# A selective scan on one core: two of sixteen products per sequence move from VectorE to GpSimd

## What is computed

```
xc = silu(causal depthwise convolution of in_proj(chunk))      # 128 channels
dt = softplus(...xc...);  B, C = projections of xc             # 16 states each
A  = -exp(A_log)
for t in range(L):
    h = exp(dt[t] * A) * h + (dt[t] * xc[t]) * B[t]            # 128 channels x 16 states
    y[t] = sum over states of h * C[t]
out = out_proj((y + xc * D) * silu(z))
```

## Time and profile before

| | before |
|---|---|
| median of three runs | 4575.1 us |
| span of the profiled execution | 4583.2 us |
| VectorE busy | 4234.4 us |
| GpSimd busy | 3430.4 us |
| ScalarE busy | 2572.6 us |
| TensorE, matmuls | 3800.3 us |
| mean granted TensorE clock | 0.921 |
| DMA moved | 752.46 MB, mean 164 GB/s |

### The profile page before, as it was taken

One profiled execution on the slowest core, in us unless ns is written; L12 is line 12 of the kernel. 1 busy time (PEld: TensorE's weight loads), 2 busy tenths in 40 slices (PEclk: granted clock), 3 DMA queues, 4 the chain that ended last, 5 costly groups with the idle time before them and its releaser, 6 DMA issues. The chain is left out here.

```text
span 4583.2 us, 51269 instructions
## 1 busy us (share of the span) xinstructions
PE 3800.3 (83%) x13584; PEld 1249.4 (27%) x13584; DVE 4234.4 (92%) x3519; ACT 2572.6 (56%) x3144; POOL 3430.4 (75%) x2085
## 2 busy tenths in 40 slices
PE   3787888888788887988888888888888878888886
PEld 2222323223232222322223232222322223232221
DVE  2699998999999999999999999999999999999997
ACT  2465565655556565565655656555565655656553
POOL 2577777777778787787777877777787777878775
PEclk8898998989999898998989999898999989989998
DMA  1567575675757757576675756757576675766764
GB/s 45 142 158 189 142 197 151 178 184 143 179 148 188 180 154 181 150 183 169 174 179 145 192 146 184 187 138 192 136 186 172 162 181 145 188 160 176 189 160 115
DMA packets 217783, 752.46 MB, mean 164 GB/s; under 512 B 27400, under 2 KB 28816, under 8 KB 213392
## 3 DMA queue, kind: packets, MB, share of 16 engines
q1 hardware_dynamic: 217488, 748.91, 63.3%
HBM read 639.75 MB, written 75.50 MB: 156 GB/s over the span
## 5 line engine op out<-in xcount | busy, mean ns | idle before, releaser
L590 POOL TENSOR_TENSOR state<-state,c_all 128x1024 f32<-128x1024 f32 x1024 | 2399.3, 2359 | 368.8 <-DVE state L960 348.8
L960 DVE TENSOR_TENSOR_SCAN state<-dtb,ub 128x1024 f32<-128x1024 f32 x1024 | 2341.0, 2286 | 51.6 <-ACT dtb L764 5.9
L1184 PE MATMUL ub<-u,spr 64*128 64x512 f32 x4096 | 1313.2, 698 | 454.5 <-DVE state L960 428.8
L764 ACT ACTIVATE dtb<-dtb,a_neg 128x1024 f32<-128x1024 f32 x1024 | 1154.5, 1141 | 537.3 <-DMA dtb<-dt_scratch 480.2
L951 DVE TENSOR_TENSOR ub<-ub,b_all 128x1024 f32<-128x1024 f32 x1024 | 1242.0, 1213 | 63.0 <-issue 30.3
L1184 PEld LDWEIGHTS ub<-u,spr 64*128 64x128 f32 x4096 | 357.4, 199 | 1288.7 <-DVE state L960 887.8
L1200 PE MATMUL yp<-state,gat 128*32 128x512 f32 x4096 | 607.3, 668 | 6.1 <-POOL state L590 6.1
L1053 PE MATMUL mb<-xs,wtap 128*128 128x512 f32 x512 | 244.4, 620 | 19.2 <-DMA xs<-xn 10.6
L657 ACT ACTIVATE e_x<-mb,col 128x512 f32<-128x512 f32 x128 | 88.0, 688 | 259.2 <-PE mb L1067 259.2
L665 ACT ACTIVATE dt<-mb 128x512 f32<-128x512 f32 x128 | 76.2, 595 | 279.4 <-PE mb L1084 279.1
L1067 PE MATMUL mb<-xc,wdt 128*128 128x512 f32 x256 | 160.5, 713 | 58.1 <-DVE ym L841 38.7
(11 more groups left out here) (130 smaller groups left out, 4657.6 us busy)
## 6 DMA issues: line engine op xcount, KB each, us to landing
dtb<-dt_scratch SPq DMA_DIRECT2D x1024, 512.0 KB, 4.8
xs<-xn SPq DMA_DIRECT2D x128, 256.0 KB, 5.2
b_all<-bc_scratch SPq DMA_DIRECT2D x64, 512.0 KB, 6.3
c_all<-bc_scratch SPq DMA_DIRECT2D x64, 512.0 KB, 7.7
xt<-in_x SPq DMA_DIRECT2D x16, 1024.0 KB, 6.9
x_scratch<-xt SPq DMA_DIRECT2D x16, 1024.0 KB, 6.9
dt_scratch<-dt SPq DMA_DIRECT2D x64, 256.0 KB, 3.4
dt_scratch<-dt SPq DMA_DIRECT2D x128, 128.0 KB, 3.7
```

The costliest lines, as they stand in the source:

```text
L590: pool.tensor_tensor(v, v, c_all[:, c % 2, :], ALU.mult).then_inc(gated, 1)
L764: act.activation(dtb[:, k, :], dtb[:, k, :], ACT.Exp, scale=a_neg[:, GROUP[g]:GROUP[g] + 1]).then_inc(decayed, 1)
L960: dve.tensor_tensor_scan(state[:, g % STATES, :], dtb[:, k, :], ub[:, g % 2, :], 0.0, ALU.mult, ALU.add).then_inc(scanned, 1)
L1184: last = pe.matmul(ub[:, g % 2, h * HALF:(h + 1) * HALF], spr[lo:lo + TURN, GROUP[g] % 8, :], u[lo:lo + TURN, c % 2, h * HALF:(h + 1) * HA ...
```

## The change

Units 6 and 14 of each sequence (`POOLED`) no longer use TensorE's spread and VectorE's multiply. SP stores u of their 8 channels into a new scratch in HBM at step 27 of the sequence before (`store_u`, four DMAs of 16 KB), and loads it back repeated for the 16 states into a new buffer `bxs` in SBUF (`load_pooled`): for unit 6 in slot 0, for unit 14 in slot 6, after the scan that read `bxs` last. GpSimd multiplies `bxs` by B in place, after gate 4 for unit 6 and after gate 12 for unit 14. The decay of these units is written to the free half 0 of `ub` in PSUM and not in place, which it may only do when unit 4 or 12 has been scanned; so the scan reads the decay from PSUM and the product from SBUF. `made` counts the multiplies that VectorE still makes, for the semaphores. The diff, its unchanged lines cut:

```diff
SEQ_STEPS = 2 * NU
+POOLED = (6, 14)
 NT = L // P
...
 POOL_SEQ = {3: ["prep_clamp_x"], 5: ["prep_silu_x"], 16: ["prep_dd"], 24: ["own_clamp_z"], 31: ["own_silu_z"]}
-SP_SEQ = {19: ["prep_bc_store"], 22: ["prep_bc_load"], 23: ["prep_store"]}
+SP_SEQ = {19: ["prep_bc_store"], 22: ["prep_bc_load"], 23: ["prep_store"], 27: ["prep_u_store"]}
 PE_BATCH = {(0, 11): ["a_group0"], (0, 12): ["post_out"], (0, 26): ["a_norm0"], (0, 28): ["a_norm1"],
...
+def made(g):
+    return g - sum(q < g for q in POOLED)
+PER_SEQ = made(NU)
 class Banks:
...
     dt_s = nc.dram_tensor("dt_scratch", (2, P, L), F32).ap()
+    u_s = nc.dram_tensor("u_scratch", (2, len(POOLED), 8, L), F32).ap()
     banks = Banks()
...
         u = sb("u", [P, 2, L])
+        bxs = sb("bxs", [P, L])
         xc = sb("xc", [P, 2, L])
...
         s_dtb = [sem(f"dt_broadcast{k}") for k in range(RING)]
+        s_ust = sem("u_stored")
+        s_bxs = sem("u_for_pool")
+        bxs_done = sem("bx_by_pool")
         ub_full = sem("u_broadcast")
...
                 await_(s_bcst, 32 * (m + 1))
-                await_(bx_done, 16 * (m - 1))
+                await_(bx_done, PER_SEQ * (m - 1))
                 await_(gated, 16 * (m - 1))
...
                     sp.dma_start(dst[:, par, :], src).then_inc(done, 16)
+            def store_u(kind, b, c):
+                par = (c + 1) % 2
+                for q in range(2):
+                    bank, use = banks(kind, b, (f"prep_dt{q}", c))
+                    await_(m_free[bank], use)
+                for i, g in enumerate(POOLED):
+                    for h in range(2):
+                        lo = (8 * GROUP[g] + h * TURN) % P
+                        sp.dma_start(u_s[par, i, :, h * HALF:(h + 1) * HALF],
+                                     u[lo:lo + 8, par, h * HALF:(h + 1) * HALF]).then_inc(s_ust, 16)
+            def load_pooled(b, c, i):
+                m = 4 * b + c
+                n = 16 * m + POOLED[i - 1] if i else 16 * (m - 1) + POOLED[-1]
+                await_(scanned, n + 1)
+                if i == 0:
+                    await_(s_ust, 32 * len(POOLED) * (m + 1))
+                sp.dma_start(bxs[:], u_s[c % 2, i].partition_broadcast(NS)).then_inc(s_bxs, 16)
...
                     store_dt(4 * b + c + 1, (c + 1) % 2)
+                elif name == "prep_u_store":
+                    store_u(kind, b, c)
                 elif name == "x_in":
...
                             load_unit(b + 1, 0, ahead_g)
+                        if g == 0:
+                            load_pooled(b, c, 0)
+                        if g in POOLED[:-1]:
+                            load_pooled(b, c, POOLED.index(g) + 1)
...
                 load_unit(0, 0, g)
+            store_u("pro", -1, NC - 1)
             turn(FIRST, 0)
...
+            def multiply(b, c, g):
+                m = 4 * b + c
+                i = POOLED.index(g)
+                if i == 0:
+                    pool.wait_ge(s_ball, 16 * (m + 1))
+                    hold_here(pool)
+                pool.wait_ge(s_bxs, 16 * (len(POOLED) * m + i + 1))
+                pool.tensor_tensor(bxs[:], bxs[:], b_all[:, c % 2, :], ALU.mult).then_inc(bxs_done, 1)
             def gate(b, c, g):
...
                         gate(b, c, g)
+                        if g + 2 in POOLED:
+                            multiply(b, c, g + 2)
                         for name in plan(POOL_SEQ, POOL_BATCH, kind, c, 2 * g + 1):
...
                 k = g % RING
+                dst = dtb[:, k, :]
+                if g in POOLED:
+                    act.wait_ge(scanned, 64 * b + 16 * c + g - 1)
+                    dst = ub[:, g % 2, :]
                 act.wait_ge(s_dtb[k], 16 * (16 * b + 4 * c + g // RING + 1))
-                act.activation(dtb[:, k, :], dtb[:, k, :], ACT.Exp, scale=a_neg[:, GROUP[g]:GROUP[g] + 1]).then_inc(decayed, 1)
+                act.activation(dst, dtb[:, k, :], ACT.Exp, scale=a_neg[:, GROUP[g]:GROUP[g] + 1]).then_inc(decayed, 1)
...
                     dve.wait_ge(dt_copied, 2 * m + h + 1)
+                    if kind != "pro":
+                        dve.wait_ge(s_ust, 32 * len(POOLED) * m)
+                        hold_here(dve)
                     dve.tensor_tensor(u[:, par, cut], mb[:, bank, :], xc[:, par, cut], ALU.mult).then_inc(m_free[bank], 1)
...
-                n = 64 * b + 16 * c + g
+                n = PER_SEQ * (4 * b + c) + made(g)
                 if g == 0:
...
                 k = g % RING
-                dve.wait_ge(bx_done, n + 1)
+                if g in POOLED:
+                    dve.wait_ge(bxs_done, len(POOLED) * (4 * b + c) + POOLED.index(g) + 1)
+                    decay, bx = ub[:, g % 2, :], bxs[:]
+                else:
+                    dve.wait_ge(bx_done, PER_SEQ * (4 * b + c) + made(g) + 1)
+                    decay, bx = dtb[:, k, :], ub[:, g % 2, :]
                 dve.wait_ge(decayed, n + 1)
                 at_least(dve, summed, n - STATES + 1)
-                dve.tensor_tensor_scan(state[:, g % STATES, :], dtb[:, k, :], ub[:, g % 2, :], 0.0,
-                                       ALU.mult, ALU.add).then_inc(scanned, 1)
+                dve.tensor_tensor_scan(state[:, g % STATES, :], decay, bx, 0.0, ALU.mult, ALU.add).then_inc(scanned, 1)
...
                     for g in range(NU):
-                        multiply(b, c, g)
+                        if g not in POOLED:
+                            multiply(b, c, g)
                         for name in plan(DVE_SEQ, DVE_BATCH, kind, c, 2 * g):
...
+                if g in POOLED:
+                    return
                 n = 64 * b + 16 * c + g
```

## The result

The changed kernel takes 5055.2 us, the median of four runs (5049.5 to 5059.6), against 4576.1 for the kernel before: ratio 1.104, 95% interval 1.102 to 1.107. The forecast was 4963 (4870 to 5045). The direction, the mechanism and nearly every stall were as forecast, but the time lies 92 us above the forecast and 10 above the range. A cost that none of the steps had in view makes up 57 us of the miss. The mean granted TensorE clock is 0.869, against 0.921 before.

A forecast was written before the change was run, and what follows sets the result against it. VectorE, busy 92% of 4583.2 us, was taken as the path; late products cost 24.8 us a turn, 388 in all, so span 4971 and, 8 us below it, 4963 us, 8.5% slower; range 4870 to 5045.

The forecast's parts named there:

- The eight places: Scans 6 and 14 of four sequences: each loses time if GpSimd's product comes late, else gains at most 1.24 us.
- the sum: Eight places give 24.8 us a turn, 372 over fifteen turns, 16 for the last: span 4583.2 to 4971 us.
- the rival of the grown chain: Before gate 12: TensorE's lower clock at own_z and ScalarE slip add 1.1 us in all four sequences, 5033 us; 10%.
- what leaves VectorE: Units 6 and 14 lose their multiply, 128 in all, saving 1.24 us each, 159 us if nothing were waited for.
- The decay in PSUM: ScalarE's Exp stays 1.14 us; at unit 14 it delays z's exponentials, +0.5 us in sequences 2 and 3.
- the hand-over from product to scan: From GpSimd's product to the scan at units 6 and 14: 0.07 us, taken from a scan's end to a waiting gate.
- DMA and queues: Loads land in 4.8 us, hidden; four stores cost SP about 0.5 us each in slot 13, nothing lost.
- Given back: Rival: engines catch up in VectorE's stalls, returning 63 us in sequence 2's queue or 60 of idle time; 4840 or 4902; 14%.
- GpSimd is on time: Rival at gates 4 and 12: no backlog ahead of them, 6.7 us a turn left as gain, 4468 us; 4%.
- Scans and gates hinder one another: Rival: every pooled scan waits for a GpSimd gate, up to 302 us, 5265 us; 2%.

The follow-up runs named there:

- e1: The changed kernel with the two semaphores for spread and VectorE's multiply counting 16 per sequence again; 4997.9 us, ratio 1.093 to the kernel before.
- e4: As e1, but GpSimd multiplies for units 6 and 14 after gates 2 and 10 instead of 4 and 12; 4530.9 us, ratio 0.990.
- e3: As e1, but GpSimd doesn't multiply u by B in units 6 and 14, the scan takes the loaded u directly; 4532.5 us, ratio 0.991.
- e2: The kernel before, with VectorE's multiply semaphore counting 2 per unit, so its wait needs its own register calculation, ahead of the waits; 4586.8 us, ratio 1.003.
- e7: The changed kernel with its own counts, the wait for the decay put ahead of the wait for the product in each scan; 4999.8 us, ratio 1.092.
- e5: As e4, but the decay of units 6 and 14 is written in SBUF, so pooled scans read both operands there; 4615.0 us, ratio 1.009.

## Why the prediction was right or wrong

**The eight places: right.** Net per turn, from the scans of e1, which has no gap to blur them:

| place | forecast | e1 |
|---|---|---|
| sequence 0, units 6, 14 | 0, +3.5 | -0.9, +3.5 |
| sequence 1, units 6, 14 | +0.1, +7.3 | +0.8, +7.3 |
| sequence 2, units 6, 14 | +4.7, +3.8 | +4.8, +3.6 |
| sequence 3, units 6, 14 | +1.6, +3.8 | +1.3, +3.6 |
| sum | 24.8 | 24.0 |
| whole turn | 24.8 | 25.6 |

In sequence 0, unit 6, scan 6 does come 0.9 us earlier, and the skip sum behind it takes back only 0.2 of them; another 0.6 are lost ahead of scan 13, where VectorE waits for ScalarE's dt. The forecast of 0 for this place was wrong by 0.9, and the turn hides it. Between the places the turn has 1.6 us more, a balance of terms that the sum had at nothing: +2.0 behind scan 15 of sequence 1, +0.8 ahead of scan 2 of sequence 2 and +0.6 ahead of scan 13 of sequence 0, against 1.9 that stalls gave back.

**The 2.0 us are TensorE's clock, which I hadn't named at this place.** Behind scan 15 of sequence 1 VectorE waits for a projection of eight passes on TensorE. In one turn of the kernel before and of e1:

```profile
2227.45 3.70 PE L1155 MATMUL mb<-cd,wp 128*128 128x512 f32 x8
```

```profile
2419.50 5.75 PE L1223 MATMUL mb<-cd,wp 128*128 128x512 f32 x8 [8.28 <-DVE xn L981]
...
2425.28 0.75 DVE L981 SCALAR_TENSOR_TENSOR xn<-mb,pb,xn 128x512 f32<-128x512 f32 x1 [1.08 <-PE mb L1223]
```

The projection doesn't start later: 1.7 us ahead of scan 15 before, 1.8 in e1. It lasts longer. Before, all fourteen loop turns have 3.70 us with a granted clock of 1.00. In e1 it is 6.2 us on average at 0.60, so mostly the lower of the two levels (1.2 and 2.4 GHz), after TensorE has stood idle for 6 to 8.3 us under the stall at scan 14; in e4, without the stall, it is 3.70 at 1.00 again. So the rival of the grown chain had the right mechanism and the wrong place.

**The register: the term that was missing.** This is the step that failed. The paragraph on what leaves VectorE counted an instruction gone and looked for waits that were added; it didn't ask what the new counts (`PER_SEQ`, `made`) do to the waits that stay. That was in the diff, in the two lines of `scan`. So the forecast had this term at nothing; the runs gave it 57 us (5055.2 to 4997.9), and without it the time lies inside the range.

**The rest of the miss, 35 us.** The span of e1 is 4994.3, the sum said 4971. The fourteen loop turns cost 0.8 us more each (12 us), the first image 1.8, and the last image 25.6 in place of 16 (10 us). Of these 25.6 the eight places are 19.7, with one product early as forecast (sequence 3, unit 6: -1.1); the other 6 lie between and behind them, where I had taken nothing. The other 12 us are the step from span to median: the runs of before lay 8 us under their profiled span, those of e1 lie 4 over it. That offset doesn't carry over; a single profiled run can lie on either side of the median.

**The decay in PSUM.** It took 1.12 us instead of the 1.14 of the earlier trace rows. The Trainium skill (ScalarE: Activation LUTs, Step-by-step) says that this form is faster; the trace agrees, by 26 ns (1115 against 1141 ns for the decays into SBUF in the same run). Exp z1 started 2.04 us after scan 12 in the changed kernel, 1.79 before: +0.25, not +0.5. Half of that term was too much. What made up for it: the hand-over from product to scan is 0.18 us, not the 0.07 that I took from the gates:

```profile
2583.97 2.34 POOL L633 TENSOR_TENSOR bxs<-bxs,b_all 128x1024 f32<-128x1024 f32 x1
...
2586.50 2.29 DVE L1026 TENSOR_TENSOR_SCAN state<-ub,bxs 128x1024 f32<-128x1024 f32 x1 [4.61 <-ACT dtb L822]
```

The product ends at 2586.31. The row names ScalarE as the releaser, but its last decay had ended at 2586.49 and was that of another unit; GpSimd's product is what the scan waited for. The page's 458.5 us are too small by such rows, which is why the sum over all releasers, 503, is the better figure.

**DMA and queues: right.** The loads of u land in 6.2 us and no wait for them appears on GpSimd; the four stores go out in 1.29 us, not 2.

**The rivals.** "Given back" was real, but small: in e1 three stretches in which VectorE had waited for TensorE are shorter by 0.9, 0.7 and 0.3 us a turn, 1.9 in all, and other terms outweigh them. It was large in the other direction: in e3 and e4 115 of the 159 us gained were lost again. "GpSimd is on time" was priced at 4468; with the product early it is 4531. Scans and gates hinder one another only with both operands in SBUF, so not in this kernel. The chain before gate 12 grew by 0.25 us, not by 1.1: the clock did fall in these stretches, from 0.91 to 0.81 over units 12 to 15 of sequence 0 and from 1.00, 0.89 and 0.85 to about 0.78 in the others, but its lower level reached few of own_z's passes (629 ns on average against 614) and met the projection behind scan 14 instead.

## What to carry to other kernels

Work given to an idle engine is worth what its place in that engine's order makes of it: the same product cost 422 us two slots ahead of its scan and gained 45 four slots ahead. A stall also reaches an engine that only waits: TensorE's clock fell in the stalls, and VectorE paid for that later in the turn. When a change gives two semaphores different counts, look at the order of waits in the loop: no register calculation should stand behind a wait that is met late, or it begins only when that wait is over. And price a saving on the bounding engine down to its next meeting with the others; here less than a third of it stayed.

## What the runs showed of the hardware that I had not expected

- A register calculation that carries a wait for the instruction before it adds 0.155 us from multiply to scan (1.24 to 1.40); ahead of the waits it adds nothing (e2). A last-met wait in an instruction of its own ahead of the scan, with no calculation behind it, adds 0.05 (e7, 1.30).
- A scan with two operands in SBUF and a gate on GpSimd hold each other up: 3.38 us instead of 2.28 for the scan and 2.53 instead of 2.36 for the gate, on average (e5 against e4).
- After 8.28 us of idle time TensorE's eight passes took 5.75 us at a granted clock of 0.64, instead of 3.70 at 1.00 (e1 and before).
- From the end of a GpSimd product to the scan that waits for it there are 0.18 to 0.19 us; from a scan's end to a waiting gate 0.08 (changed kernel).
